# MLP's first product for 14 of 16 token blocks by seven products on pairs of blocks

## The chip, the cores and the metric

One core of a Trainium2 chip runs the whole kernel, a layer with a normalisation, a state space scan, a gelu MLP and a second, FP4-quantised MLP. The metric is the time on the device in microseconds, as the median of several runs. The engines are TensorE (PE in the profile, with its weight loads PEld), VectorE (DVE), ScalarE (ACT), GpSimd (POOL) and SyncE (SP), which here issues all the DMAs, in order.

## The reference

For 2 x 4096 tokens of 512 channels, in float32 (`_L0_ffn_ref` is the quantised MLP, with widths 512, 1408, 512):

```python
xn = _layernorm(x, axis=-1)
x = x + _L0_attn_ref(xn, ...) + _L0_ffn_ref(xn, w_gate, w_up, w_down)

def _L0_attn_ref(x, A_ssm, B_ssm, C_ssm, D_ssm, scale1, scale2, w1, b1, w2, b2):
    x = x + ssm_scan(rmsnorm(x, scale1), A_ssm, B_ssm, C_ssm, D_ssm)
    h = rmsnorm(x, scale2)
    h = jax.nn.gelu(h @ w1 + b1, approximate=False) @ w2 + b2   # w1 512 x 2048, w2 2048 x 512
    return x + h
```

## The kernel before

The tokens are 64 tiles of 128. The first 1742 us do the quantised MLP and the scan and leave two things in DRAM: r_Z (a tile's residual and second MLP) and r_Y (the scan's result). Then comes the MLP stage, the one that changes. Its tokens are 16 blocks of 512 (NB), and its weights are 16 pieces of 128 hidden channels. Every float32 operand of TensorE is split into a high part (rounded to fp32r) and the remainder, and a product takes three passes (PASSES): high with high, high with low, low with high. `Wp[f][0]` and `Wp[f][1]` are high and low of piece f, with w1's part in `[:, 0]` and w2's in `[:, 1]`, and all 16 pieces stay in SBUF.

In each step n = 16 b + f of a loop over the whole stage, `mlp1(n)` (L880) makes 12 matmuls of 512 columns, 4 pieces of the 512 channels by 3 passes, into bank 7 or 4. ScalarE takes gelu of it into `gf` (`gelu`, L1491). VectorE casts that to G2's high part (L1237) and subtracts to get the low part (L1239, `gelu_parts`). Two steps later `mlp2(n)` (L896) makes 12 matmuls, 4 tiles by 3 passes, into banks 0 to 3, which are summed over a block's 16 steps. After f = 15 `result` (L1250) adds the tile's residual, and SP stores it.

Beside that, each tile of the next block is prepared (`prepare`, at steps set by `mlp_steps`). `pre_load` and `z_load` load x, r_Y and r_Z; VectorE's `tile_add` normalises x and adds Y (L1193, L1197); ScalarE squares it for a sum (`tile_square`, L1456); VectorE's `tile_root` is a chain of 11 one-column operations and one scaling (L1203 to L1209); GpSimd's `tile_z` makes the residual with two sums of 128x512 (L1631, L1634), and tile_root's scaling waits for them. `quadrants` stores the tile to DRAM and loads it back with its 32x32 pieces in other places (four DMAs of 128-byte pieces), so that VectorE's 32x32 transpose (L1221) gives the whole transpose, from which `tile_high` and `tile_low` make hT. Block 0 also waits for each piece's weights: `w_high` on ScalarE (L1450) and `w_low` on VectorE (L1188) split piece n + 2 in step n.

Each engine runs a program in order, written out by hand: a wait of one instruction holds all that stands behind it on the same engine. Semaphores give the order between engines.

## Time and profile before

| | us |
|---|---|
| median of 3 runs | 3132.64 |
| lowest, highest | 3131.24, 3133.47 |
| span of the profiled execution | 3132.1 |
| MLP stage from its third first product to TensorE's last matmul | 1742.8 to 3128.9 |

| stretch | TensorE busy | VectorE | ScalarE | GpSimd |
|---|---|---|---|---|
| MLP stage, 1386.1 us | 1383.8 | 664.4 | 286.0 | 160.8 |
| one block of it, 87.04 us | 87.04 | 42.16 | 17.74 | 10.79 |

The profiled execution's span stands half a microsecond below the median of the runs. A matmul's row in the trace is longer than the distance to the next, since matmuls overlap in the array; so the distance of starts is the cost of one. A row of VectorE or GpSimd that took longer than others of its kind waited inside the instruction. "Idle before" in a row ends with the instruction that released it.

### The profile page before, as it was taken

What the parts mean: (1) busy time and instruction counts of PE and PEld (TensorE: products, weight loads), DVE (VectorE), ACT (ScalarE), POOL (GpSimd) and SP (SyncE); (2) the same over time, 40 slices, a digit from 0 to 9 for tenths busy, and PEclk for the clock granted to TensorE, in tenths of its full rate; (3) what the DMA queues carried; (4) which work ended last, traced back from release to release, by engine and by line L of the source; (5) the groups of instructions that cost most, each with busy time, mean ns of one, the idle gap of its engine ahead of it and who ended that gap; (6) DMA issues with size and microseconds to landing.
All of it is one profiled execution on the core that took longest, in us unless ns stands there. A gap on an engine that the chain in (4) does not pass through costs nothing.

```text
span 3132.1 us, 43122 instructions
## 1 busy us (share of the span) xinstructions
PE 3053.1 (97%) x14861; PEld 2472.6 (79%) x14861; DVE 2040.8 (65%) x4427; ACT 1086.7 (35%) x1910; POOL 1149.5 (37%) x1097
## 2 busy tenths in 40 slices
PE   5899999999999999999999999999999999999999
PEld 3678888888877777777777788888888888888887
DVE  8798898987777776767777754444445444444442
ACT  5345655644544343343422422212222122221221
POOL 7556656655555545545554210110111111111000
PEclk9999999999999999999999999999999999999999
DMA  4133434356766666666644533333333333333320
GB/s 128 44 88 91 116 114 120 95 137 183 181 180 174 161 155 174 159 161 168 168 95 98 128 72 72 75 73 72 77 68 80 75 68 71 72 74 74 71 61 14
DMA packets 865577, 335.58 MB, mean 107 GB/s; under 512 B 680400, under 2 KB 771792, under 8 KB 862800
## 3 DMA queue, kind: packets, MB, share of 16 engines
q1 hardware_dynamic: 865360, 332.83, 43.4%
q8 instruction: 119, 1.95, 0.3%
q14 instruction: 98, 0.80, 0.1%
HBM read 225.21 MB, written 107.51 MB: 106 GB/s over the span
## 4 chain that ended last, share of the span: by engine, by line
PE 70%; DVE 15%; issue 5%; POOL 5%; ACT 2%; DMA 2%; SPq 1%; DVEq 0%; POOLq 0%; ACTq 0%
PE bank L880 22%; PE bank L896 22%; PE bank L757 14%; PE bank L779 7%; DVE qs L1000 3%; POOL qa L1547 2%; DVE qa L1017 2%; PE bank L820 2%; DVE qs L1011 2%; DVE qa L973 2%; POOL qa L1541 1%; DVE qb L1025 1%; PE bank L727 1%; PE bank L828 1%; DVE sg L965 1%
## 5 line engine op out<-in xcount | busy, mean ns | idle before, releaser
L880 PE MATMUL bank<-hT,Wp 128*128 128x512 f32 x3072 | 739.6, 390 | 2.2 <-DVE Wp L1188 2.2
L896 PE MATMUL bank<-Wp,G 128*128 128x512 f32 x3072 | 737.6, 389 | 0.0
L880 PEld LDWEIGHTS bank<-hT,Wp 128*128 128x128 f32 x3072 | 577.5, 188 | 122.6 <-issue 2.6
L896 PEld LDWEIGHTS bank<-Wp,G 128*128 128x128 f32 x3072 | 576.6, 188 | 119.9
L757 PE MATMUL bank<-XT,Wg 128*128 128x512 f32 (+1 forms) x2148 | 524.6, 393 | 6.8 <-DVE Wd L1032 6.8
L757 PE MATMUL bank<-XT,Wu 128*128 128x512 f32 (+1 forms) x2148 | 515.7, 389 | 15.9 <-DVE sg L965 15.7
L779 PE MATMUL bank<-Wd,HT 128*128 128x512 f32 x2112 | 515.4, 393 | 6.3 <-POOL HT L1555 5.0
L1237 DVE CAST G<-gf 128x512 fp32r<-128x512 f32 x256 | 110.8, 433 | 599.2 <-PE bank L896 580.0
L757 PEld LDWEIGHTS bank<-XT,Wu 128*128 128x128 f32 x2148 | 401.1, 190 | 106.7 <-issue 25.8
L779 PEld LDWEIGHTS bank<-Wd,HT 128*128 128x128 f32 x2112 | 391.9, 188 | 105.6 <-issue 15.4
L757 PEld LDWEIGHTS bank<-XT,Wg 128*128 128x128 f32 x2148 | 398.7, 190 | 95.9 <-DVE Wd L1032 8.8
L1547 POOL TENSOR_TENSOR qa<-qb,qs 128x512 f32<-128x512 f32 (+2 forms) x277 | 308.2, 1113 | 343.8 <-DVE qb L1025 341.4
L1491 ACT ACTIVATE gf<-bank,vec 128x512 f32<-128x512 f32 x256 | 176.3, 689 | 604.6 <-PE bank L880 603.2
L1555 POOL TENSOR_TENSOR HT<-qb,HT 128x512 fp32r<-128x512 f32 (+1 forms) x179 | 229.6, 1283 | 242.3 <-ACT HT L1331 242.1
L1631 POOL TENSOR_TENSOR zx<-zl,b2r 128x512 f32<-128x512 f32 x64 | 88.9, 1389 | 609.7 <-DMA out_dram<-zx 527.9
L1541 POOL TENSOR_TENSOR qa<-qa,qs 128x512 f32<-128x512 f32 (+1 forms) x243 | 262.8, 1082 | 109.2 <-DVE qs L1005 109.2
L1634 POOL TENSOR_TENSOR zx<-zx,xl 128x512 f32<-128x512 f32 x64 | 82.8, 1293 | 505.0 <-DVE xl L1197 504.3
L1331 ACT ACTIVATE HT<-qb 128x512 fp32r<-128x512 f32 (+1 forms) x179 | 112.1, 626 | 413.2 <-DVE qb L979 413.1
L1017 DVE SCALAR_TENSOR_TENSOR qa<-qb,qa 128x512 f32<-128x512 f32 (+2 forms) x149 | 120.7, 810 | 141.0 <-ACT qb L1303 140.8
L1239 DVE TENSOR_TENSOR G<-gf,G 128x512 fp32r<-128x512 f32 x256 | 178.3, 696 | 8.8
L1338 ACT ACTIVATE sg<-bank 128x512 f32<-128x512 f32 (+1 forms) x179 | 105.5, 590 | 204.9 <-PE bank L757 201.4
L1000 DVE TENSOR_REDUCE qs<-qa 128x32 f32<-128x512 f32 (+1 forms) x243 | 165.2, 680 | 8.3
(121 smaller groups left out, 2828.3 us busy)
## 6 DMA issues: line engine op xcount, KB each, us to landing
px<-in_L_attn_x_dram SPq DMA_DIRECT2D x128, 256.0 KB, 3.3
xin<-in_L_attn_x_dram SPq DMA_DIRECT2D x128, 256.0 KB, 3.3
sT<-r_K SPq DMA_DIRECT2D x128, 256.0 KB, 4.2
r_Z<-xin SPq DMA_DIRECT2D x64, 256.0 KB, 2.5
r_U<-ub SPq DMA_DIRECT2D x16, 1024.0 KB, 6.6
sU<-r_U SPq DMA_DIRECT2D x32, 512.0 KB, 5.0
r_Y<-sY SPq DMA_DIRECT2D x16, 1024.0 KB, 5.7
xl<-in_L_attn_x_dram SPq DMA_DIRECT2D x64, 256.0 KB, 3.1
```

The lines of the kernel that those rows point to most:

```text
L757: ins = e.matmul(bk[:, 0:n], W[wh][:, k, :], inputs(xh, w, k), start=(k == 0 and p_ == 0), stop=(k == KD - 1 and p_ == 2))
L779: ins = e.matmul(DNB[t % 4][:], HT[hh][:, w % 2, a * P:(a + 1) * P], Wd[wh][:, f, :], start=(w == first(n) and p_ == 0), stop=(w == last(n ...
L880: ins = e.matmul(bk[:], Wp[f][wh][:, 0, k * P:(k + 1) * P], hT[xh][b % 2][:, k, :], start=(k == 0 and p_ == 0), stop=(k == KD - 1 and p_ = ...
L896: ins = e.matmul(ACC[j][:], G2[gh][:, n % 2, j * P:(j + 1) * P], Wp[f][wh][:, 1, :], start=(f == 0 and p_ == 0), stop=(f == 15 and p_ == 2))
L1000: e.tensor_reduce(s_, blk(job_in(m)), AX, ALU.max, apply_absolute_value=True).then_inc(s_mx, 1)
L1017: e.scalar_tensor_tensor(Aa, Bb, FLOOR, Aa, ALU.max, ALU.add).then_inc(s_t, 1)
L1239: e.tensor_tensor(G2[1][:, n % 2], gf[:, n % 2], G2[0][:, n % 2].bitcast(F32), ALU.subtract).then_inc(s_glo, 1)
L1331: e.activation(HT[0][:, w % 2, 0:n], qb[:, m % 2, 0:n], ACT.Copy).then_inc(s_hh, 1)
L1491: e.activation(gf[:, n % 2], PB[n % 2][:], ACT.Gelu, bias=vec[:, f:f + 1]).then_inc(s_gl, 1)
L1541: e.tensor_tensor(blk(qa[:, m % 4, 0:n]), blk(job_in(m)), bc(qs[:, m % 4, 1, 0:n // 16], n // 16), ALU.mult).then_inc(s_pa, 1)
L1547: e.tensor_tensor(blk(qa[:, m % 4, 0:n]), blk(qb[:, m % 2, 0:n]), bc(qs[:, m % 4, 0, 0:n // 16], n // 16), ALU.mult).then_inc(s_ph, 1)
L1555: e.tensor_tensor(lo, qb[:, m % 2, 0:n], hi.bitcast(F32), ALU.subtract).then_inc(s_hl, 1)
```

## The change

Blocks 0 and 1 (NB1 = 2) keep the old loop. The other 14 blocks become 7 pairs (PAIRS). For a pair and a unit u, which is a pair of weight pieces 2u and 2u + 1, the first product is a 2x2 block product: the weights are A11, A12, A21, A22 (two pieces by two halves of the 512 channels), the activations B11, B12, B21, B22 (two halves of the channels by two blocks of 512 tokens). Strassen's scheme in Winograd's form makes the four results with seven products instead of eight. It needs four sums of weights (S1 to S4) and four of activations (T1 to T4). Each product is 2 k-halves by 3 passes, 6 matmuls.

**Weights.** In steps 3 to 25 sixteen rounds (`combine_steps`) make the eight weight operands: load of w1, scaling by scale2 on ScalarE, four 128x128 sums on GpSimd (`combine_sums`), high parts on ScalarE (`combine_high`, 128x1024), remainders on GpSimd (`combine_low`, 128x1024), store to r_A in pieces of 512 bytes. There are two buffers wt, one wh and one wl. Later each product's weights, 256 KB, are loaded from r_A into a ring of 14 places.

**Activations.** Each tile is normalised with one unit of the pair before (the first eight in steps 14 to 26, `early_steps`), its residual is summed in place in `zl` and stored to r_Q, the tile to r_N. SP loads two tiles at a time with the pieces moved (`quarters`), VectorE transposes (`conv_turn`), sums into banks (`conv_sums`), ScalarE converts, VectorE and GpSimd subtract (`conv_low`). For a later pair all that lies in `rest`; for the first it lies in steps 26 to 33.

**A unit.** Seven products go into banks 4 to 7, several of them into a bank that is read between two products; VectorE adds the parts (u2, u3, and three results), ScalarE takes four gelus. Between the products stand pieces of the even block's second product for the unit before, into banks 0 to 3. The odd block's second product can't have a bank meanwhile, so its gelus are kept in SBUF and it gets a stretch of its own, `rest`: 16 parts for it and the last 2 of the even block, into banks 4 to 7. The remainder of a gelu's cast moves from VectorE to GpSimd (`second_rest`), and there are three buffers for it. Bank 0 to 3 are scratch for the sums of the next pair once the even block's results are out.

```diff
@@ mlp_steps: the old loop ends with block 1
+    if b + 1 >= NB1:
+        return []
...
+STEPS = ((A11, B11, 4), (S2, T2, 5), (S3, T3, 6), (A12, B21, 4), (S1, T1, 7), (A22, T4, 6), (S4, B22, 7))
+OPENS = (0, 1, 2, 4)
+SECOND = [(0, f) for f in range(14)] + [(1, 0), (1, 1), (0, 14), (0, 15)] + [(1, f) for f in range(2, 16)]
...
+def combine_steps(n):
+    return [k for k in range(16) if 3 + 4 * k // 3 == n]
+def early_steps(n):
+    return [(OLD + r, part) for part in (1, 0) for r in range(8) if 14 + 3 * r // 2 + part == n]
@@ sync_program
+            def unit(c, u):
+                g, o = 8 * c + u, OLD + 8 * (c + 1) + u
+                more = c + 1 < PAIRS
+                for k in range(7):
+                    if g + 2 < 8 * PAIRS:
+                        e.wait_ge(s_p, 7 * g + k + 1)
+                        ring_load(7 * (g + 2) + k)
+                    if u == 7 and k == 1 and more:
+                        quarters(c + 1, 0)
+                    if k == 2 and more:
+                        store_sum(o)
...
+                    if k == 4 and more:
+                        store_normed(o)
+                        z_load(o + 1)
+                    if k == 5 and more and u < 6:
+                        pre_load(o + 2)
...
+            combine_load(0)
+            combine_load(1)
-            for n in range(2, 16 * NB + 2):
+            for n in range(2, 16 * NB1 + 2):
                 if n == 2:
                     z_out(NT - 2)
                     z_out(NT - 1)
+                for k in combine_steps(n - 2):
+                    combine_store(k)
+                for k in combine_steps(n - 1):
+                    combine_load(k + 2)
@@ tensor_program
+            def product(c, u, k):
...
+                elif k == 0:
+                    e.wait_ge(s_gc, 5 * (g - 1) + 2)
...
+                elif k == 5:
+                    e.wait_ge(s_add, 5 * g + 2)
+                elif k == 6:
+                    e.wait_ge(s_add, 5 * g + 3)
+                e.wait_ge(d_ring[q % 14], RING_0 + 16 * (q // 14 + 1))
+                for kt in range(2):
+                    for p_, (xh, wh_) in enumerate(PASSES):
+                        ins = e.matmul(bank[bk][:], ring(q)[:, 256 * wh_ + P * kt:256 * wh_ + P * kt + P],
+                                       combined(b, xh)[:, kt], start=(k in OPENS and kt == 0 and p_ == 0),
+                                       stop=(kt == 1 and p_ == 2), skip_group_check=True)
...
+            def unit(c, u):
+                after = [[(0, 0)], [(0, 1)], [(0, 2), (0, 3)], [(1, 0)], [(1, 1)], [(1, 2)], [(1, 3)]]
+                for k in range(7):
+                    product(c, u, k)
+                    if u:
+                        for a, j in after[k]:
+                            second(c, 2 * (u - 1) + a, j)
@@ vector_program
+            def second_part(c, i):
...
+                if q >= 3:
+                    e.wait_ge(s_m2, used((q - 3) // 32, (q - 3) % 32))
...
+                e.tensor_copy(second_high(q), gelued(half, f)).then_inc(s_gh, 1)
+            def conv_sums(c, i):
...
+                e.tensor_tensor(ba[:, 0:256], HB[:, 0:256], HA[:, 0:256], ALU.subtract).then_inc(s_ts, 1)
+                e.tensor_tensor(ba[:, 256:512], HB[:, 256:512], HB[:, 0:256], ALU.subtract).then_inc(s_ts, 1)
+                e.wait_ge(s_ts, n + 1)
+                e.tensor_tensor(bb[:, 0:256], HB[:, 256:512], ba[:, 0:256], ALU.subtract).then_inc(s_ts, 1)
+                e.wait_ge(s_ts, n + 3)
+                e.tensor_tensor(bb[:, 256:512], HA[:, 256:512], bb[:, 0:256], ALU.subtract).then_inc(s_ts, 1)
+            def unit(c, u):
+                if u:
+                    second_part(c, 2 * u - 1)
+                if c + 1 < PAIRS:
+                    tile_add(o)
...
+                e.tensor_tensor(u2[:], bank[5][:], s1[:], ALU.add).then_inc(s_add, 1)
...
+                e.tensor_tensor(u3[:], bank[6][:], u2[:], ALU.add).then_inc(s_add, 1)
+                if c + 1 < PAIRS:
+                    tile_root(o)
+                second_part(c, 2 * u if u < 7 else 14)
...
+                e.tensor_tensor(gelued(1, 2 * u + 1), bank[7][:], u3[:], ALU.add).then_inc(s_add, 1)
+            def rest(c):
+                for i in range(16, 32):
+                    second_part(c, i)
+                    if i in (17, 18, 24, 26) and more:
+                        conv_turn(d, (17, 18, 24, 26).index(i))
+                    if i == 19:
+                        for j in range(4):
+                            sum_out(c, j)
+                    if i in (20, 21, 25, 28) and more:
+                        conv_sums(d, (20, 21, 25, 28).index(i))
+                    if i in (22, 23, 27, 29) and more:
+                        conv_low(d, (22, 23, 27, 29).index(i))
@@ scalar_program
+            def combine_high(k):
+                e.wait_ge(s_wsum, WSUM0 + 4 * (k + 1))
+                if k:
+                    e.wait_ge(d_wa, WA_0 + 32 * k)
...
+                e.activation(wh[:], wt[:, k % 2], ACT.Copy).then_inc(s_wah, 1)
@@ gpsimd_program
+            def combine_sums(k):
+                w = [wt[:, k % 2, i] for i in range(8)]
+                e.wait_ge(s_wsc, WSC0 + 2 * (k + 1))
+                e.tensor_tensor(w[S1], w[A21], w[A22], ALU.add).then_inc(s_wsum, 1)
+                e.tensor_tensor(w[S3], w[A11], w[A21], ALU.subtract).then_inc(s_wsum, 1)
...
+            def combine_low(k):
+                e.wait_ge(s_wah, WAH0 + k + 1)
+                e.tensor_tensor(wl[:], wt[:, k % 2], wh[:].bitcast(F32), ALU.subtract).then_inc(s_wal, 1)
+            def second_rest(c, i):
+                e.wait_ge(s_gh, q + 1)
+                e.tensor_tensor(second_low(q), gelued(half, f), second_high(q).bitcast(F32), ALU.subtract
+                                ).then_inc(s_gw, 1)
```

**Order on TensorE, inside the MLP stage.** Before, the end of one first product (L880) and the start of a second product (L896), where twelve stand in a row of each:

```order
L880 MATMUL bank<-hT,Wp_1 128x512
L880 MATMUL bank<-hT,Wp_0 128x512 x2
L880 MATMUL bank<-hT,Wp_1 128x512
L880 MATMUL bank<-hT,Wp_0 128x512
L896 MATMUL bank<-Wp_0,G 128x512
L896 MATMUL bank<-Wp_1,G 128x512
```

Now, inside a unit (L1193 is `product`, its weights in the ring `Wp_1`, its activations in HC or WH; L1215 is `second`):

```order
L1193 MATMUL bank<-HC,Wp_1 128x512 x6
L1215 MATMUL bank<-Wp_0,G 128x512
L1215 MATMUL bank<-Wp_1,G 128x512
L1215 MATMUL bank<-Wp_0,G 128x512
L1193 MATMUL bank<-WH,Wp_1 128x512 x6
```

A run of six now alternates with a run of three, and each has waits of its own.

**Order on GpSimd, in the first steps of the MLP stage.** Before, only the residuals of tiles stand there:

```order
L1555 TENSOR_TENSOR HT1<-qb,HT0 128x256
L1631 TENSOR_TENSOR zx1<-zl,b2r 128x512
L1634 TENSOR_TENSOR zx1<-zx1,xl0 128x512
L1631 TENSOR_TENSOR zx1<-zl,b2r 128x512
L1634 TENSOR_TENSOR zx1<-zx1,xl1 128x512
```

Now, with L2201 to L2206 `combine_sums`, L2210 `combine_low`, L2189 and L2192 `tile_z`:

```order
L2192 TENSOR_TENSOR zx1<-zx1,xl0 128x512
L2201 TENSOR_TENSOR wt<-wt 128x128
L2202 TENSOR_TENSOR wt<-wt 128x128
L2204 TENSOR_TENSOR wt<-wt 128x128
L2206 TENSOR_TENSOR wt<-wt 128x128
L2201 TENSOR_TENSOR wt<-wt 128x128
L2202 TENSOR_TENSOR wt<-wt 128x128
L2204 TENSOR_TENSOR wt<-wt 128x128
L2206 TENSOR_TENSOR wt<-wt 128x128
L2210 TENSOR_TENSOR wl<-wt,wh 128x1024
L2189 TENSOR_TENSOR zx1<-zl,b2r 128x512
L2192 TENSOR_TENSOR zx1<-zx1,xl1 128x512
```

Two rounds of sums and one remainder now stand between the residuals of two tiles.

**Order on VectorE, beside the second products.** Before, a step's cast and remainder, and a tile's transpose and low parts:

```order
L1237 CAST G<-gf 128x512
L1239 TENSOR_TENSOR G<-gf,G 128x512
L1221 STREAM_TRANSPOSE bank<-xl 128x512
L1224 SCALAR_TENSOR_TENSOR hT<-bank,vec,hT 128x128 x4
L1237 CAST G<-gf 128x512
```

Now, in `rest` (L1648 is `second_part`, L1600 `conv_turn`, L1696 `sum_out`, L1616 to L1621 `conv_sums`):

```order
L1648 CAST G2x<-GX 128x512
L1600 STREAM_TRANSPOSE yl<-xl 128x512
L1600 STREAM_TRANSPOSE xl<-yl 128x512
L1648 CAST G<-GX 128x512
L1696 TENSOR_TENSOR zq<-bank,zq 128x512 x2
L1696 TENSOR_TENSOR gf<-bank,gf 128x512 x2
L1648 CAST G<-GX 128x512
L1616 TENSOR_TENSOR bank<-xl,st 128x256
L1617 TENSOR_TENSOR bank<-xl 128x256
L1619 TENSOR_TENSOR bank<-xl,bank 128x256
L1621 TENSOR_TENSOR bank<-st,bank 128x256
L1648 CAST G2x<-GX 128x512
```

The casts that TensorE needs now have results, transposes and sums of the next pair between them, and no remainder.

## Rows read from the trace of the kernel before

**Rows 1.** The page: the span, TensorE's 40 slices, GB/s of all queues.
```profile
span 3132.1 us, 43122 instructions
...
PE   5899999999999999999999999999999999999999
...
GB/s 128 44 88 91 116 114 120 95 137 183 181 180 174 161 155 174 159 161 168 168 95 98 128 72 72 75 73 72 77 68 80 75 68 71 72 74 74 71 61 14
```

**Rows 2.** Stretches: length, busy PE, PEld, DVE, ACT, POOL (x), PEclk, DMA share, GB/s.
```profile
1818.96:1906.00 87.04, 87.04 (x385) 72.07 (x385) 42.16 (x113) 17.74 (x40) 10.79 (x8) 1.00 0.37 73
...
1742.80:3128.90 1386.10, 1383.84 (x6097) 1145.02 (x6095) 664.41 (x1735) 285.99 (x635) 160.80 (x120) 1.00 0.34 70
```

**Rows 3.** Timeline: start us, us, engine, line, op, tiles, count.
```profile
2002.61 2.88 PE L880 MATMUL bank<-hT,Wp 128*128 128x512 f32 x12
...
2005.33 2.88 PE L896 MATMUL bank<-Wp,G 128*128 128x512 f32 x12
2005.53 0.69 ACT L1491 ACTIVATE gf<-bank,vec 128x512 f32<-128x512 f32 x1 [4.75 <-PE bank L880]
```

**Rows 4.** Waits of the MLP stage: us in total, times, longest us.
```profile
ACT gf L1491 <- PE bank L880: 603.2, 144, 4.8
```

**Rows 5.** Groups by shape, 1600 to 3100 us: count, busy us, mean ns.
```profile
L1239 DVE TENSOR_TENSOR G<-gf,G 128x512 fp32r<-128x512 f32 x251 | 174.8, 697 | 8.6
L1491 ACT ACTIVATE gf<-bank,vec 128x512 f32<-128x512 f32 x252 | 173.5, 689 | 585.6 <-PE bank L880 584.2 <-DVE G L1239 1.4
L1237 DVE CAST G<-gf 128x512 fp32r<-128x512 f32 x251 | 108.6, 433 | 577.8 <-PE bank L896 558.6 <-ACT gf L1491 19.1
...
L1221 DVE STREAM_TRANSPOSE bank<-xl 128x512 f32<-128x512 f32 x60 | 43.2, 720 | 0.0
...
L1193 DVE TENSOR_SCALAR xl<-xl,mv,rst 128x512 f32<-128x512 f32 x64 | 36.0, 563 | 0.5 <-DMA xl<-in_L_attn_x_dram 0.5
```

**Rows 6.** Timeline: first and last of the 12 operations of tile_root.
```profile
1939.79 0.14 DVE L1203 TENSOR_SCALAR rs<-rs 128x1 f32<-128x1 f32 x1
...
1941.89 0.49 DVE L1209 TENSOR_SCALAR xl<-xl,rs 128x512 f32<-128x512 f32 x1
```

**Rows 7.** Timeline: GpSimd and VectorE together, at 1938 and at 1761.
```profile
1938.02 1.29 POOL L1631 TENSOR_TENSOR zx<-zl,b2r 128x512 f32<-128x512 f32 x1 [2.15 <-DMA zl<-r_Z]
1938.06 1.80 DVE L1239 TENSOR_TENSOR G<-gf,G 128x512 fp32r<-128x512 f32 x1
...
1761.70 1.43 POOL L1631 TENSOR_TENSOR zx<-zl,b2r 128x512 f32<-128x512 f32 x1 [1.50 <-DMA zl<-r_Z]
1761.91 1.50 DVE L1237 CAST G<-gf 128x512 fp32r<-128x512 f32 x1
```

**Rows 8.** Groups of VectorE by shape, whole run: one line, two kinds of input.
```profile
L1025 DVE SCALAR_TENSOR_TENSOR qb<-qb,qa 128x512 f32<-128x512 f32 x142 | 124.0, 873 | 4.9
...
L1025 DVE SCALAR_TENSOR_TENSOR qb<-bank,qa 128x512 f32<-128x512 f32 x125 | 84.5, 676 | 3.2
```

**Rows 9.** Groups of GpSimd by shape, whole run.
```profile
L1575 POOL TENSOR_TENSOR kR<-kR,kC 128x128 f32<-128x128 f32 x60 | 27.6, 461 | 4.6
...
L1541 POOL TENSOR_TENSOR qa<-qa,qs 128x256 f32<-128x256 f32 x6 | 3.8, 626 | 2.8 <-DVE qs L1005 2.8
```

**Rows 10.** DMA issues, to 1745 us, then 1742 to 1830: median us to landing.
```profile
r_W<-kE SPq DMA_DIRECT2D x16, 256.0 KB, 3.0
...
zl<-r_Z SPq DMA_DIRECT2D x4, 256.0 KB, 2.9
r_H<-xl SPq DMA_DIRECT2D x4, 256.0 KB, 2.0
xl<-r_H SPq DMA_DIRECT2D x16, 64.0 KB, 2.5
```

**Rows 11.** Timeline: TensorE's stall after a weight remainder; SP's four pieces.
```profile
1761.53 4.58 PE L880 MATMUL bank<-hT,Wp 128*128 128x512 f32 x12 [2.22 <-DVE Wp L1188]
...
1762.83 2.61 SPq L595 DMA_DIRECT2D xl<-r_H  x4
```

More of the change, by code:

```diff
@@ L266, in build @@
         yl1 = sbt(mctx, "yl1", [P, D])
-        for f in (8, 9, 10, 0, 1, 2, 3, 4, 5, 6, 7):
+        for f in (8, 9, 10):
+            piece(f)
+        with ExitStack() as later:
+            WH = sbt(later, "WH", [P, 8, 4 * D], F32R)
+        for f in range(8):
             piece(f)
@@ new lines, in rest @@
+            def rest(c):
+                more = c + 1 < PAIRS
+                if more:
+                    quarters(c + 1, 1)
+                residual_in(c, 2)
+                residual_in(c, 3)
+                for i in range(4):
+                    tile_result(c, i)
+                for i in range(4, 8):
+                    residual_in(c, i)
+                if more:
+                    quarters(c + 1, 2)
+                    quarters(c + 1, 3)
+                if c + 2 < PAIRS:
+                    pre_load(OLD + 8 * (c + 2))
+                    pre_load(OLD + 8 * (c + 2) + 1)
+                for i in range(4, 8):
+                    tile_result(c, i)
@@ L601, in prepare @@
                     return
[L602 removed]
+                if part == 0:
                     z_load(t + 1)
@@ new lines, in second @@
+            def second(c, i, j):
+                half, f = SECOND[i]
+                q = 32 * c + i
+                for p_, (gh, wh_) in enumerate(PASSES):
+                    if p_ == 0 and (j == 0 or i >= 30):
+                        e.wait_ge(s_gw, q + 1)
+                    if p_ == 0 and f == 0 and half == 0:
+                        if c:
+                            e.wait_ge(s_ev, 8 * (c - 1) + j + 1)
+                        else:
+                            e.wait_ge(s_o, OLD)
+                    if p_ == 0 and f == 0 and half == 1:
+                        g = 8 * c + 7
+                        if j == 0:
+                            e.wait_ge(s_gc, 5 * g + 2)
+                        else:
+                            e.wait_ge(s_add, 5 * g + (1, 4, 5)[j - 1])
+                    ins = e.matmul(bank[4 * half + j][:], (second_high(q), second_low(q))[gh][:, j * P:(j + 1) * P],
+                                   Wp[f][wh_][:, 1, :], start=(f == 0 and p_ == 0), stop=(f == 15 and p_ == 2))
+                if j == 3 and i != 30:
+                    ins.then_inc(s_m2, 1)
+                elif f == 15:
+                    ins.then_inc(s_ac2, 1)
@@ new lines, in unit, with rest @@
+            def unit(c, u):
[5 more added lines that the diff above has]
+                            second(c, 2 * (u - 1) + a, j)
+            def rest(c):
+                for i in range(14, 30):
+                    for j in range(4):
+                        second(c, i, j)
+                for j in range(4):
+                    second(c, 30, j)
+                    second(c, 31, j)
@@ L914, in tensor_program @@
             window(NW + 1)
-            for n in range(2, 16 * NB + 2):
-                if n < 16 * NB:
+            for n in range(2, 16 * NB1 + 2):
+                if n < 16 * NB1:
                     mlp1(n)
@@ L920, in tensor_program @@
                 mlp2(n - 2)
+            for c in range(PAIRS):
+                for u in range(8):
+                    unit(c, u)
+                rest(c)
         def vector_program(e):
@@ new lines, in sum_out, with rest @@
+            def sum_out(c, i):
+                if i % 4 < 3:
+                    e.wait_ge(s_ac2, 6 * c + 3 * (i // 4) + i % 4 + 1)
+                else:
+                    e.wait_ge(s_m2, used(c, 17 if i < 4 else 31))
+                e.wait_ge(d_zq[i % 4], ZQ_0 + 16 * (2 * c + i // 4 + 1))
+                e.tensor_tensor(residual(i), bank[i][:], residual(i), ALU.add).then_inc(s_ev, 1)
+            def rest(c):
+                d = c + 1
+                more = d < PAIRS
+                for i in range(16, 32):
[3 more added lines that the diff above has]
+                    if i == 19:
+                        for j in range(4):
+                            sum_out(c, j)
[3 more added lines that the diff above has]
+                        conv_low(d, (22, 23, 27, 29).index(i))
+                for j in range(4, 8):
+                    sum_out(c, j)
@@ L1292, in vector_program @@
                     prepare(t, part)
+                for o, part in early_steps(n):
+                    (tile_add, tile_root)[part](o)
+            for c in range(PAIRS):
+                for u in range(8):
+                    unit(c, u)
+                rest(c)
         def scalar_program(e):
@@ L1640, in gpsimd_program, with rest @@
+            def rest(c):
+                for i in range(16, 32):
+                    second_rest(c, i)
+                    if i in (17, 20, 25, 27) and c + 1 < PAIRS:
+                        conv_low(c + 1, (17, 20, 25, 27).index(i))
             for m in range(NJ + 3):
```

443 lines of the change are left out of this document (407 added, 36 removed).

## The prediction

> **What bounds the kernel now.** Read the 40 slices of the page first: TensorE stands at 9 in all but the first two [rows 1]. The stage that the change touches is the last 1386 us, from 1742.8 to 3128.9. There TensorE is busy 1383.8 of 1386.1 us, VectorE 664, ScalarE 286, GpSimd 161, the DMA engines a third of the time, at a granted clock of 1.00, which is the 2.4 GHz level [rows 2]. The timeline shows why no other engine matters: a group of 12 matmuls starts every 2.72 us, first product and second product in turn, with no gap at the border [rows 3]. One matmul of 512 columns thus costs 2.72/12 = 0.2267 us (the 0.39 us of a row overlaps the next). The list of waits has its longest total here: ScalarE's gelu waits 603 us for TensorE, up to 4.8 us at a time [rows 4]. TensorE itself waits once in the stage, 2.22 us, below. So each matmul less is worth 0.2267 us, as long as nothing comes late.
>
> **Matmuls removed.** A pair of blocks had 2 x 16 x 12 = 384 matmuls in its first product. Now it has 8 units of 7 products of 2 k-halves by 3 passes, 336. The second product keeps its 384. Seven pairs: 7 x 48 = 336 fewer, 336 x 0.2267 = **76.2 us less**. The transposes of activations in this stage are not on TensorE before or after.
>
> **Inside a unit.** Times are from a unit's start; a product takes 1.36 us, a piece of second product 0.68 or 1.36: in units 1 to 7, 66 matmuls, 14.96 us. Consumers start 0.43 us after the last matmul's start (12 matmuls from 2002.61, the last at 2005.10, gelu at 2005.53 [rows 3]), VectorE's a little later. VectorE: cast to 0.7, the tile's add (0.56 + 0.69 [rows 5]), at worst behind one GpSimd op of 1.29, u2 by 4.9, u3 by 6.4, root chain to 9.0 (11 small ops in 2.1 us, then 0.49) [rows 6], cast to 9.6, sum into bank 7's reader at 10.5 to 11.2; TensorE needs u3 at 10.9 for product 5 and that last sum at 12.9 for product 6. Nothing is late. Unit 0 has no second product beside it, 9.5 us: there product 6 wants the sum at 8.16, but VectorE does u3 to 5.0, the root chain to 7.65, cast to 8.1, sum to 8.8. That is 0.7 and a hop, 0.9 us, in the six pairs that prepare a next one: **+5**. The weight ring is 14 products deep and reloaded two units ahead; 7 x 256 KB and four or five transfers of the tile per 15 us is about 210 GB/s, while slices of the kernel before moved up to 183 without a full queue [rows 1], so I cost it at nothing; with that cover gone it would be tenths of a us per product.
>
> **GpSimd and VectorE share something.** In the timeline at 1938 a VectorE op with two SBUF inputs that starts 0.04 us after a GpSimd op takes 1.80 instead of 0.69, ending 0.55 after GpSimd's end; at 1761.9 a cast takes 1.50 instead of 0.43, ending 0.28 after it [rows 7]. The same line L1025 averages 873 ns with both inputs in SBUF and 676 with one in a bank [rows 8]. So ops of GpSimd and such ops of VectorE (two SBUF inputs, or a cast or scaling from SBUF to SBUF) come one after the other, and readers of a bank are free. Before this costs nothing, because GpSimd has 10.8 us of work per block of 87 [rows 2]. The change gives it much more, so this is the price to work out.
>
> **Blocks 0 and 1, with the weight sums beside them.** Steps are 5.44 us. From step 3 to step 26 (127 us) GpSimd gets 16 rounds of four 128x128 sums (0.46 each) and one 128x1024 remainder (2.38, on the line through 0.46, 0.62, 1.29 for 128, 256 and 512 columns) [rows 7, 9], 67 us, and 12 tiles by 2 x 1.29, 31 us. VectorE holds the same path for 0.28 of a cast and 0.55 of a two-input op [rows 7]: 24 x 0.83 for gelu parts, 24 x 0.55 for weight remainders, 12 x 1.2 for tiles (two scalings 0.28, one two-input op 0.55, small ops), 47 us. Together 145 in 127 us. ScalarE's conversion waits for GpSimd, and the gelu behind it in its queue has 10.88 - (2.9 + 0.69) = 7.3 us of slack [rows 3, 5]; so even a port without an idle moment leaves TensorE 145 - 127 - 7 = 11 us late. Two loops are not without idle moments. The z tile of a pair is a single buffer: load 2.9, two sums 2.6, store 2.0, issues 0.7 [rows 10], 8.2 us plus a hold of about 1, against the 8.16 us that 1.5 steps give, eight times; and one buffer of high parts must be stored (3.0, the nearest row is r_W [rows 10]) before the next conversion. I add 15: **+26**. Bounds: 0, were the sums late without anyone waiting; above, VectorE's own work per step (cast 0.43, remainder 0.69, two weight remainders 1.38, a third of a tile's 6.1) is 4.5, and with all of GpSimd's 4.1 in its way 8.6, so 3.2 x 22 - 7 = 63. Port and loops have the better evidence, so I stay nearer to the lower end.
> The queue ahead of it: the two first loads of sums stand before the last r_Z stores on SP, and the chain r_Z, GpSimd, VectorE, weight remainder already stalls TensorE 2.22 us at 1761.5 [rows 11]. Two loads of 256 KB, of which one alone lands in 2.9 us [rows 10], at about 1 us each in a row: **+2** (0 to 4).
> The pair that follows block 1: its last quarter is turned in step 32, after the remainders of gelu(31), then sums, five conversions, remainders. Laid end to end this ends 9 to 10 us after step 32 begins, when TensorE has 5.44 us of work: **+5** (3 to 15; the upper end if SP, which needs 2.61 us to issue the four pieces of one tile and so 5.2 per quarter [rows 11], is late).
>
> **The own stretch of the second product.** 216 matmuls, 49 us per pair. Each of its 16 parts must be cast (0.43) and subtracted (1.29) in the 5.2 us between the release of its buffer and its use, so VectorE may be 3.4 us late. It is also given 8 transposes (0.72 [rows 5]), 16 half sums (0.43), 12 remainders and 8 results: about 33 us with the casts, and GpSimd 29 us. Going through the queue, parts 21, 22, 26 and 30 come 0.3 to 1.1 us late, because a half sum waits for GpSimd and then the cast for both: 2.4 us; some of it falls on gaps, I take 2 by six pairs, **+12** (0 to 36). The last results and stores after the last matmul are as many as before, at no change.
> The Trainium skill (GPSIMD Engine Reference, 4.1 Engine selection) says that two-input elementwise work belongs on VectorE, GpSimd being about twice slower; rows agree (1.29 against 0.69). By that rule the remainders' move to GpSimd is what loads the shared path, and the 12 us would be near 0 had they stayed; the sum would read 3094.
>
> **Sum.** 3132.1 - 76.2 + 5 + 26 + 2 + 5 + 12 = 3105.9 on the profiled execution; the median of the runs lies 0.5 above its span, so **3106.4**.
>
> **Rivals.** *All covered* (0.22): the rounds of sums have no one waiting in time, holds fall into gaps, only unit 0 and the handover cost, 3132.6 - 76.2 + 5 + 3 = 3064 to some 3085. For it: VectorE and ScalarE idle more than half of the stage [rows 2]. Against: orders are fixed, a wait of one blocks all behind it. *Late quarters* (0.08): in the second stretch VectorE waits in its queue for pieces of 128 bytes that SP issues in 5.2 us per two tiles [rows 11]; if they land 4 us later than the 2.5 of [rows 10], each pair loses 6 instead of 2: 3106 + 24 to 3140. The Trainium skill (DMA: Bandwidth & Descriptors, Specifications) wants at least 512 bytes per piece. The trace shows 2.5 us to landing with pieces of 128 bytes, in a lightly loaded queue. *VectorE bound, slower* (0.10): in blocks 0 and 1 each small op of the root chain meets another GpSimd op, VectorE takes 8.6 us per step, TensorE follows: 3106.4 + 63 - 26 = 3143. It turns slower than before once these blocks lose more than 52 us, 2.4 us per step. *Broken cadence, not what it says* (0.05): groups are now 3 and 6 matmuls with a wait each instead of 12; if a border costs 0.08 us, some 110 per pair make 60 us and 3166. Against: borders between groups of 12 with two or three waits cost 0 [rows 3]. *Forecast* (0.55): 3085 to 3126.
>
> A measurement of this kernel can tell 0.2%, 6.3 us, from no change. Faster than 3126.4 (forecast, all covered and a little of the late quarters): 0.80; within: 0.07; slower: 0.13. The range that leaves out less than two in ten is 3070 to 3136.
>
> **What would show it.** Twelve matmuls in 2.72 us inside a unit (else the cadence fails). Units 1 to 7 of 14.96 us, unit 0 about 10.4, waiting before product 6 for the sum after the root. In blocks 0 and 1 GpSimd busy about 90%, small VectorE ops of 0.5 to 2 us, TensorE idle some 28 us in all, waits naming gelu or conversions. In the own stretch 49 us plus about 2, waits for GpSimd's remainder. The prediction is wrong if these blocks take under 190 us or over 215, or if rest stretches exceed 53.

## The result and the profile after

The changed kernel takes 3200.8 us (median of four runs, 3198.2 to 3203.5) where the kernel before takes 3132.6 beside it: a ratio of 1.0217, 95% interval 1.0204 to 1.0230. It is 68 us slower; 3106.4 and a range of 3070 to 3136 were forecast. Sign and range are both wrong. The working below is on the profiled executions, 3197.4 us against 3132.1, so 65.3 us are to be found. Of all executions one, of e11 below, ran at a granted clock of 0.565 and took 5004 us; it stands in no figure here.

The page of the kernel after: span, TensorE's busy tenths in 40 slices, its granted clock.

```profile
span 3197.4 us, 44061 instructions
...
PE   5899999999999999999999666899999999999999
...
PEclk9999999999999999999999878999999999999999
```

Before, all slices but the first two stood at 9 [rows 1]. Now slices 23 to 26, which are blocks 0 and 1 of the MLP, stand at 6, 6, 6 and 8, and the granted clock dips with them. The rest is as full as before. Four of the ten stretches by windows, and their sum from 1740 to 2040 (length, busy time of PE, PEld, DVE, ACT, POOL with counts, granted clock, DMA share, GB/s):

```profile
1740.00:1760.00 20.00, 18.96 (x84) 15.39 (x82) 9.02 (x24) 5.66 (x12) 1.27 (x1) 1.00 0.75 211
1760.00:1790.00 30.00, 21.51 (x72) 16.46 (x72) 18.41 (x28) 6.98 (x12) 17.01 (x17) 0.83 0.45 121
...
1850.00:1880.00 30.00, 12.89 (x49) 9.66 (x48) 12.69 (x20) 8.10 (x19) 9.96 (x9) 0.76 0.51 128
1880.00:1910.00 30.00, 23.65 (x91) 18.62 (x89) 14.59 (x38) 5.91 (x13) 11.58 (x16) 0.90 0.72 172
...
sum 300.00, PE 205.67 PEld 160.50 DVE 157.00 ACT 80.50 POOL 118.47; mean PE 20.57 PEld 16.05 DVE 15.70 ACT 8.05 POOL 11.85
```

No engine is full there. GpSimd, forecast at 90%, is busy 10 to 17 of 30 us in each stretch from 1760 to 2000, and 118 of the 300. So something other than an engine's full load sets the time. Measured from the trace by the starts of matmuls:

| part | before | after | forecast | difference |
|---|---|---|---|---|
| blocks 0 and 1, first mlp1 to first product, 769 starts | 182.6 | 302.3 | 190 to 215 | +119.7 |
| 336 matmuls less, at 0.2267 | | | -76.2 | -76.2 |
| eight units of the first pair (113.56 without a wait) | | 119.99 | 113.6 + 0.9 + 5 | +6.4 |
| eight units of pairs 2 to 6 | | 114.01 each | 114.5 | +0.45 each |
| own stretches (49.64 without a wait) | | 50.9 to 52.7 | 51.6 | +13.4 in six |

-76.2 + 119.7 + 6.4 + 2.3 + 13.4 = 65.6, which is the 65.3 within rounding. All but one of the lines came out near their forecast; one line, blocks 0 and 1, holds the whole miss. "Without a wait" is the number of matmuls times 0.2267. Against an unbroken cadence these blocks lose 128.3 us (before: 8.5, of which 4.4 are matmuls of the stage ahead that stand between the first groups, as they do now): 99.9 in 23 gaps of more than 1 us, and 27.7 in 138 matmuls that start 0.3 to 1 us after the one before, by median 0.427, where 0.2267 is the cadence.

The list of waits, 1730 to 2035 (us in total, times, longest):

```profile
ACT wh L1981 <- DMA r_A<-wl: 115.5, 14, 16.2
POOL wl L2210 <- ACT wh L1981: 83.6, 14, 13.0
PEld bank L1142 <- ACT gf L1964: 58.3, 10, 11.0
...
PE bank L1142 <- ACT gf L1964: 38.2, 7, 10.6
ACT wt L1973 <- DMA wt<-in_L_attn_w_dram: 35.3, 8, 11.4
...
PE bank L1142 <- DVE Wp L1527: 27.4, 7, 8.1
```

SP's own waits, 1738 to 2030, begin with its load of the next round's weights, which stands behind the round's remainder:

```profile
SPq L751 <- POOL wl L2210: 88.3, 12, 8.7
```

The stores of a round, from issue to landing:

```profile
r_A<-wh SPq DMA_DIRECT2D x16, 512.0 KB, 4.2
r_A<-wl SPq DMA_DIRECT2D x16, 512.0 KB, 5.2
```

Before, ScalarE's one long wait in this stage was for TensorE [rows 4]; now TensorE waits most for ScalarE's gelu, and ScalarE waits for a store. One turn of the loop, from the timeline (start, us, engine, line, operation):

```profile
1792.54 1.06 ACT L1981 ACTIVATE wh<-wt 128x1024 fp32r<-128x1024 f32 x1 [12.72 <-DMA r_A<-wl]
...
1793.67 2.35 POOL L2210 TENSOR_TENSOR wl<-wt,wh 128x1024 fp32r<-128x1024 f32 x1 [13.05 <-ACT wh L1981]
...
1794.50 1.16 ACT L1923 ACTIVATE Wp<-Wr 128x512 fp32r<-128x512 f32 x2
...
1795.54 0.70 ACT L1964 ACTIVATE gf<-bank,vec 128x512 f32<-128x512 f32 x1
...
1796.05 0.37 SPq L751 DMA_DIRECT2D wt<-in_L_attn_w_dram  x1
...
1796.46 0.47 SPq L695 DMA_DIRECT2D xl<-in_L_attn_x_dram  x1
...
1796.71 4.89 PE L1142 MATMUL bank<-hT,Wp 128*128 128x512 f32 x12 [6.93 <-DVE Wp L1527]
...
1796.97 2.57 SPq L699 DMA_DIRECT2D yl<-r_Y  x2
...
1799.59 1.02 SPq L759 DMA_DIRECT2D r_A<-wh  x1
1800.65 2.00 SPq L759 DMA_DIRECT2D r_A<-wl  x1
...
1806.31 1.06 ACT L1981 ACTIVATE wh<-wt 128x1024 fp32r<-128x1024 f32 x1 [6.34 <-DMA r_A<-wl]
```

Read it as a ring. Conversion 1.1, GpSimd's remainder 2.4, SP's issues that stand ahead of the stores in program order (a load of weights, xl, two pieces of yl) 3.5, the high store's issue 1.0, and from the low store's issue to its landing 5.7: 13.8 us from one conversion to the next. The program asks for one in 4/3 steps, 7.25 us; 16 turns at 6.5 too many make 105 us. This turn is not an odd one: the 16 conversions stand 14.8 us apart in the mean. The conversion stands in ScalarE's queue ahead of the next gelu, and ahead of the high part of block 0's next weight piece (L1923), whose remainder the 6.93 us of this turn are waiting for; neither can start while it waits. And the group after a stall takes 4.89 us instead of 2.88: its granted clock is 0.56, and its matmuls start 0.427 us apart, which is the 1.2 GHz level. The trace of before had one such restart, 4.58 us after a 2.22 us stall [rows 11].

### The profile page after: what moved, and what is told of

It is laid out like the page before. It is cut to its first block and busy times, and to the rows that moved or that the text cites. A ratio compares the mean times of both kernels' runs of the same rounds, so it can differ in the third digit from the quotient of the medians.

```text
span 3197.4 us, 44061 instructions
## 1 busy us (share of the span) xinstructions
PE 3016.1 (94%) x14525; PEld 2427.6 (76%) x14525; DVE 2179.4 (68%) x4455; ACT 1156.7 (36%) x1930; POOL 1599.9 (50%) x1457
## 5 line engine op out<-in xcount | busy, mean ns | idle before, releaser
L1019 PE MATMUL bank<-XT,Wu 128*128 128x512 f32 (+1 forms) x2148 | 516.4, 390 | 15.3 <-DVE sg L1304 14.8
L1215 PE MATMUL bank<-Wp,G 128*128 128x512 f32 x1800 | 456.9, 391 | 5.3 <-POOL G L2226 5.2
L1193 PE MATMUL bank<-HC,Wp 128*128 128x512 f32 x1680 | 423.5, 391 | 2.8 <-POOL WH L2219 2.8
L1215 PEld LDWEIGHTS bank<-Wp,G 128*128 128x128 f32 x1800 | 336.9, 188 | 79.7 <-POOL G L2226 10.5
L1193 PEld LDWEIGHTS bank<-HC,Wp 128*128 128x128 f32 x1680 | 316.8, 189 | 68.7 <-POOL WH L2219 3.2
L2226 POOL TENSOR_TENSOR G<-gf,G 128x512 fp32r<-128x512 f32 x75 | 103.3, 1378 | 301.6 <-DVE G L1648 301.6
L1215 PE MATMUL bank<-Wp,G2x 128*128 128x512 f32 x888 | 229.2, 391 | 3.3 <-POOL G2x L2226 3.3
L1215 PEld LDWEIGHTS bank<-Wp,G2x 128*128 128x128 f32 x888 | 166.2, 188 | 39.9 <-POOL G2x L2226 5.8
L1142 PE MATMUL bank<-hT,Wp 128*128 128x512 f32 x384 | 115.5, 460 | 81.3 <-ACT gf L1964 38.2
L1193 PE MATMUL bank<-WH,Wp 128*128 128x512 f32 x672 | 171.3, 391 | 5.0 <-DVE GX L1674 2.6
```

The source lines that it names most:

```text
L1019: ins = e.matmul(bk[:, 0:n], W[wh][:, k, :], inputs(xh, w, k), start=(k == 0 and p_ == 0), stop=(k == KD - 1 and p_ == 2))
L1142: ins = e.matmul(bk[:], Wp[f][wh][:, 0, k * P:(k + 1) * P], hT[xh][b % 2][:, k, :], start=(k == 0 and p_ == 0), stop=(k == KD - 1 and p_ = ...
L1193: ins = e.matmul(bank[bk][:], ring(q)[:, 256 * wh_ + P * kt:256 * wh_ + P * kt + P], combined(b, xh)[:, kt], start=(k in OPENS and kt == 0 ...
L1215: ins = e.matmul(bank[4 * half + j][:], (second_high(q), second_low(q))[gh][:, j * P:(j + 1) * P], Wp[f][wh_][:, 1, :], start=(f == 0 and ...
```

## The experiments

Theory *loop*: the ring above sets the time. Theory *port*: GpSimd's work on the path that it shares with VectorE does. All kernels are timed against the kernel before on the same chip (3132.4 to 3133.5); not all stand on one chip. "Lost" is what a profiled execution's matmuls lose against 0.2267 us each up to the first product.

**e1, no rounds.** combine_load, combine_store, combine_scale, combine_sums, combine_high and combine_low are not called; the ring is filled with other data and the waits are changed to match (as in e2):

```
-                for k in combine_steps(n):
-                    combine_sums(k)
-                for k in combine_steps(n - 1):
-                    combine_low(k)
```

> Left out: all sixteen rounds of weight sums (loads, scalings, sums, conversions, remainders, stores); the ring reads as many bytes from another tensor, so the products have wrong weights. Loop theory (each round goes once around ScalarE's conversion, GpSimd's remainder, SP's stores and their landing before the next may begin, about 14 us, and gelu stands behind it in ScalarE's queue) and port theory (the 145 us of GpSimd and VectorE work that exclude each other) both say: blocks 0 and 1 fall from 302 us to about 190, the rest stays, total 3080 to 3095. If it stays above 3150, neither is the cause and the new order of tiles or the ring is.

3086.2 us, ratio 0.985 (0.983 to 0.987); blocks 0 and 1 take 188.1 us, lost 14.1. So everything outside the rounds holds: 47 us faster than the kernel before, and the rounds cost 115 us, more than the whole miss of 94.

**e2, rounds without stores.**

```
-                for k in combine_steps(n - 2):
-                    combine_store(k)
...
-                e.dma_start(ring(q).bitcast(F32), r_A[q // 7 % 8, STEPS[q % 7][0]]).then_inc(d_ring[q % 14], 16)
+                e.dma_start(ring(q).bitcast(F32), r_Z[q % 56]).then_inc(d_ring[q % 14], 16)
...
-                    e.wait_ge(d_wa, WA_0 + 32 * k)
+                    e.wait_ge(s_wal, WAL0 + k)
```

> Left out: the stores of the weight operands and the waits for their landing; all sums, conversions and remainders stay, the ring reads as many bytes from another tensor (wrong weights). Loop theory: without the landing a round takes some 5 us and nobody waits for it, blocks 0 and 1 take 190 to 210 us, total 3085 to 3105. Port theory: GpSimd's and VectorE's work is the same, so blocks 0 and 1 stay at 280 us or more, total above 3175.

3132.8 us, ratio 0.9997 (0.9987 to 1.0007); lost 59.3. Neither theory's number: the stores cost 68 us, and the rounds without them still 47 against e1.

**e3, stores first.** SP issues a round's stores a step earlier, ahead of the loads of weights and of the tile:

```
-                for k in combine_steps(n - 2):
+                for k in combine_steps(n - 1):
                     combine_store(k)
-                for k in combine_steps(n - 1):
                     combine_load(k + 2)
```

> Same work and result; on SP the two stores of a round now stand right behind its remainder, one step earlier and ahead of the tile's stores and loads. Loop theory: 3 to 5 us of SP's own detour leave each of 16 rounds, 50 to 80 us in all: 3120 to 3150. Port theory: no change, 3195 to 3205.

3158.6 us, 1.0082 (1.0067 to 1.0097); lost 87.9. Issuing the stores ahead of SP's other work gives back 42 us, where 50 to 80 were expected. ScalarE's longest wait is now for the next load:

```profile
ACT wt L1972 <- DMA wt<-in_L_attn_w_dram: 58.4, 9, 10.5
...
ACT wh L1980 <- DMA r_A<-wl: 31.7, 5, 8.9
```

**e4, more buffers.** Three wt with the remainder written in place of the sums, two wh, loads one round further ahead, and the stores one step earlier, but behind SP's work for the tile in that step. As the remainder lies in wt, a load must now wait until that buffer's store has landed:

```
-        wt = sbt(mctx, "wt", [P, 2, 8, P])
-        wh = sbt(mctx, "wh", [P, 8, P], F32R)
-        wl = sbt(mctx, "wl", [P, 8, P], F32R)
+        wt = sbt(mctx, "wt", [P, 3, 8, P])
+        wh = [whx, sbt(mctx, "wh", [P, 8, P], F32R)]
...
-                if k >= 2:
-                    e.wait_ge(s_wal, WAL0 + k - 1)
...
+                if k >= 3:
+                    e.wait_ge(d_sl[k % 3], SL[k % 3] + 16 * (k // 3))
```

> Same work and result; two buffers for the high parts, three for the sums with the remainder written in place, so a conversion waits for the store of two rounds before, not of the last. Loop theory: the loop is no longer closed over a landing; blocks 0 and 1 take 195 to 215 us, total 3095 to 3115, faster than the kernel before. Port theory: as before, 3185 or more.

3157.7 us, 1.0074 (1.0057 to 1.0090); lost 86.1. A miss for the loop theory in its simple form. The wait for r_A is gone from the top of ScalarE's list, but the change put a new one on SP, in front of the next load (the last row is SP's own list), and the loads and the tile's z come late in its place.

```profile
ACT wt L1984 <- DMA wt<-in_L_attn_w_dram: 50.7, 9, 10.4
POOL zl L2203 <- DMA zl<-r_Z: 42.6, 6, 13.7
```

```profile
SPq L755 <- DMA r_A<-wt: 39.8, 10, 5.1
```

**e5 and e6, small operations.** To part the engines' time from the waits, all operations of a round work on 8 columns of each matrix, without stores (e5) and with them (e6, where round 0 stays whole). Of e5:

```
-                w = [wt[:, k % 2, i] for i in range(8)]
+                w = [wt[:, k % 2, i, 0:8] for i in range(8)]
...
-                e.activation(wh[:], wt[:, k % 2], ACT.Copy).then_inc(s_wah, 1)
+                e.activation(wh[:, :, 0:8], wt[:, k % 2, :, 0:8], ACT.Copy).then_inc(s_wah, 1)
```

> As e2 (the rounds without stores of the weight parts; the ring of the products is filled with other data), but every operation of a round works on 8 columns of each 128x128 matrix instead of 128: the loads (512 KB of w1 twice halved, one per round), all instructions, all waits and their places in the queues stay. What is left of the rounds is their chain of waits; what goes is the time of GpSimd, ScalarE and VectorE in them and with it the shared path. e2 had 3132.8 and lost 233.4 - 188.1 = 45 us against e1 in blocks 0 and 1. Port theory (GpSimd's 67 us of sums and remainders and the holds that they give to VectorE are the 45): these blocks take 188 to 195 us, the kernel 3086 to 3095. Chain theory (weights loaded late by an SP queue that stands in other waits, and ScalarE's scaling standing in front of the next gelu, are the 45): the blocks take 220 to 233, the kernel 3118 to 3133. In between, each has the share that is read off.

> The changed kernel with both stores of 512 KB per round and their waits, but with the operations of rounds 1 to 15 on 8 columns of each matrix (round 0 whole; the stored weights are then not the sums, and the output not the reference's). It is the store loop alone. Loop theory: a round still needs the high store (4.2), the low store (5.2) and SP's detours, some 10 to 11 of the 14 us, so 16 rounds take 165 us where the steps give 127, and the blocks lose 35 to 50 us against e1: 223 to 238 us, kernel 3120 to 3140. Port theory (the losses are holds that let the stores seem late): 188 to 200 us, kernel 3086 to 3100.

e5: 3097.0 us, 0.989 (0.9873 to 0.9906), lost 25.4, 2 us above what port asked and far from the chain's 3118. e6: 3166.3 us, 1.0106 (1.0089 to 1.0123), lost 93.8, more than the loop theory asked. Of e6, the list of waits and the timeline of the ring, now with next to no work in it:

```profile
ACT wh L1982 <- DMA r_A<-wl: 108.4, 14, 13.5
```

```profile
1839.36 2.28 SPq L759 DMA_DIRECT2D r_A<-wh  x1
...
1841.68 0.58 SPq L759 DMA_DIRECT2D r_A<-wl  x1
1846.70 0.26 ACT L1982 ACTIVATE wh<-wt 128x64 fp32r<-128x64 f32 x1 [7.46 <-DMA r_A<-wl]
1846.87 0.67 ACT L1964 ACTIVATE gf<-bank,vec 128x512 f32<-128x512 f32 x1
...
1853.51 0.26 ACT L1982 ACTIVATE wh<-wt 128x64 fp32r<-128x64 f32 x1 [5.97 <-DMA r_A<-wl]
```

A conversion of 0.26 us waits 7.46 us for a store, and the gelu starts behind it. Four kernels now make a square, in medians:

| | operations small | operations whole | difference |
|---|---|---|---|
| no stores | 3097.0 (e5) | 3132.8 (e2) | 35.8 |
| stores | 3166.3 (e6) | 3200.8 (changed) | 34.5 |
| difference | 69.3 | 68.0 | |

The two causes simply add, within the noise. From e1's 3086.2 (two executions, 7 us apart): loads, waits and places in the queues 10.8, the operations' time about 35, the stores about 68.

**e9, GpSimd's time alone.** e5 with operations of GpSimd behind each round's small ones that nobody waits for:

```
+                for i in range(4 if k else 0):
+                    idle_work(wl[:, i, 8:P], wl[:, i + 4, 8:P].bitcast(F32))
...
+                if k:
+                    idle_work(wl[:, :, 8:P], wl[:, :, 8:P].bitcast(F32))
```

> e5 (rounds without stores, all their operations on 8 columns) with GpSimd's time given back: behind each round's small sums four operations of 128x120 and behind its small remainder one of 128x960, with two SBUF inputs, on data that nobody waits for. The round's own chain stays short; ScalarE's scalings and conversion stay small. e2 - e5 was 36 us. Port theory (GpSimd's time, in its own queue and on the path that it shares with VectorE, costs TensorE the 36): e9 at 3125 to 3137. Chain theory (the 36 come because each round's operations stand one behind the other until its conversion, and the conversion and scalings of full size hold the gelu behind them): e9 within 8 us of e5, 3097 to 3105.

3121.3 us (3116.8 to 3124.6), 0.9959 (0.9945 to 0.9974); lost 47.3. Between the two forecasts, nearer to port: some 24 of the 36 us are GpSimd's time (22 by what the profiled executions lost), the other 12 need the whole chain or ScalarE's share. How it reaches TensorE stands in its timeline:

```profile
1790.54 2.08 POOL L2201 TENSOR_TENSOR wl<-wl 128x960 fp32r<-128x960 f32 x1
...
1791.01 2.16 DVE L1535 TENSOR_TENSOR xl<-xl,yl 128x512 f32<-128x512 f32 x1
...
1793.20 0.63 ACT L1928 ACTIVATE yl<-xl 128x512 f32<-128x512 f32 x1 [3.84 <-DVE xl L1535]
...
1793.83 1.13 ACT L1922 ACTIVATE Wp<-Wr 128x512 fp32r<-128x512 f32 x2
...
1794.47 1.26 POOL L2191 TENSOR_TENSOR zx<-zx,xl 128x512 f32<-128x512 f32 x1
1794.48 2.41 DVE L1526 TENSOR_TENSOR Wp<-Wr,Wp 128x512 fp32r<-128x512 f32 x2 [1.31 <-ACT Wp L1922]
...
1796.43 4.46 PE L1141 MATMUL bank<-hT,Wp 128*128 128x512 f32 x12 [2.01 <-DVE Wp L1526]
...
1800.02 1.79 POOL L2201 TENSOR_TENSOR wl<-wl 128x960 fp32r<-128x960 f32 x1
...
1800.11 1.72 DVE L1291 SCALAR_TENSOR_TENSOR rs<-rs 128x1 f32<-128x1 f32 x1
```

VectorE's add takes 2.16 instead of 0.69 behind 2.08 us of GpSimd. ScalarE's square waits for the add, and the high part of a weight piece (L1922) stands behind the square. Its two remainders on VectorE then meet the tile's own sum on GpSimd (L2191), take 2.41 instead of 1.3, and TensorE stands 2.01 us for the second.

**e7 and e8, one size changed.** Four blocks go the old way instead of two, and the 16 rounds come one in 18.1 us; e8 is the same without rounds:

```
-NB1 = 2
+NB1 = 4
...
-    return [k for k in range(16) if 3 + 4 * k // 3 == n]
+    return [k for k in range(16) if 3 + 10 * k // 3 == n]
```

> One size changed: four blocks instead of two go the old way, and the same 16 rounds come one in 10/3 steps (18.1 us) instead of one in 4/3 (7.25); six pairs instead of seven go by seven products. Matmuls removed: 6 x 48 = 288, 65.3 us. e1 stood 29.8 us over 3132.6 - 76.2 - ... with its 7 pairs (11.7 in the rest stretches, 6.4 at the first pair, some 5 in blocks 0 and 1, the rest in unit 0 and around); with 6 pairs about 28. Loop theory (a round needs 14 us and 7.25 is too short): the rounds cost 0 to 8 us, kernel 3095 to 3105. A price per round whatever the pace (holds that TensorE pays each time): 115 us as in the changed kernel, 3205; or as in e2 47, 3142.

> e7 without the rounds (ring filled with other data), as e1 is to the changed kernel; the output is not the reference's. Both theories: 3132.6 - 65.3 + 28 = 3095, within 3090 to 3100. It is there for e7: the difference of the two is what 16 rounds cost at the slower pace.

e8 3095.6 us, as expected. e7 3118.7 us, 0.996 (0.9946 to 0.9974), lost 39.3 over four blocks against 16.6 in e8. The same 16 rounds cost 23 us instead of 115, so the price is set by the pace, and not by a fee per round; but 23 is more than the 0 to 8 of the loop theory. Most rounds of e7 also lie behind block 0, where no weights are split. That isn't what saves it: the second half of block 0, with splitting, loses 45 us in the changed kernel and 5.5 in e7, and block 1, without any, loses 57 in the changed kernel.

**e10, e11, e12: what is left at the slower pace.** e10 is e7 with e3's order of SP, e11 is e7 with e4's buffers, and e12 is e10 with

```
-    return [k for k in range(16) if 3 + 10 * k // 3 == n]
+    return [k for k in range(16) if 3 + 8 * k // 3 == n]
```

> e7 (four old blocks, rounds at 18.1 us) with SP's stores of a round put straight behind its remainder, ahead of the tile's issues, as e3 is to the changed kernel. In e7 16 rounds cost 23 us. Loop theory: at 18.1 us a round is no longer bound by its store loop but still late now and then where SP's detours fall in (ScalarE waited 3 times, 6.8 us, for r_A); the order takes these away, 5 to 12 us: 3107 to 3114. Port theory: the 23 us are GpSimd's holds, nothing changes: 3116 to 3121.

> e7 with e4's buffers: three for the weights of a round with the remainder in place, two for the high parts, loads a round earlier. Nothing then waits for a store or a load at this pace. Loop theory: 8 to 15 of the 23 us go, 3104 to 3111. Port theory: 3116 to 3121.

> e10 with a round every 8/3 steps (14.5 us) instead of 10/3 (18.1), so that the 16 rounds are done by step 43, before the eight early tiles and the conversions of the first pair begin at step 46. If the cost comes from rounds and early tiles meeting (port, SP, or ScalarE's queue), it is below e10: 3098 to 3106. If it comes from the pace of the loop (14.5 is near the 14 that a round took), it is above e10: 3115 to 3130.

e10: 3112.7 us, 0.9938 (0.9921 to 0.9955), lost 34.8. This is in the loop theory's range. e11: 3118.8 us, ratio 0.995 (0.9934 to 0.9967), lost 39.5, no gain over e7: the loop theory's forecast for it failed. e12: 3106.6 us, 0.9916 (0.9901 to 0.9931), lost 28.4, where 3098 to 3106 were expected if rounds and early tiles got in each other's way, and 3115 or more if the pace alone counted. A faster round, done before the first pair's tiles begin, is better than a slower one beside them: in the last of the four blocks e12 loses 7.1 us, e10 17.1 and e8, without rounds, 7.3. e12 beats both kernels: 27 us under the kernel before and 94 under the changed one. In it the store is all but out of the list of waits, the gelu follows its conversion at once, and what still holds TensorE now and then is a late operation of VectorE:

```profile
ACT wh L1982 <- DMA r_A<-wl: 3.6, 3, 2.0
```

```profile
1824.10 1.06 ACT L1982 ACTIVATE wh<-wt 128x1024 fp32r<-128x1024 f32 x1 [2.40 <-POOL wt L2210]
...
1825.23 2.37 POOL L2214 TENSOR_TENSOR wl<-wt,wh 128x1024 fp32r<-128x1024 f32 x1 [1.17 <-ACT wh L1982]
1826.06 0.70 ACT L1965 ACTIVATE gf<-bank,vec 128x512 f32<-128x512 f32 x1
...
1827.40 3.02 PE L1142 MATMUL bank<-hT,Wp 128*128 128x512 f32 x12 [0.91 <-DVE hT L1563]
```

## Why the prediction was wrong, step by step

**Right.** The cadence: 0.2267 us a matmul also in groups of 3 and 6, with no cost at the borders. Groups of the kernel after from 2041 us on (count, busy us, mean ns, idle before):

```profile
L1215 PE MATMUL bank<-Wp,G 128*128 128x512 f32 x1800 | 456.9, 391 | 5.3 <-POOL G L2226 5.2
L1193 PE MATMUL bank<-HC,Wp 128*128 128x512 f32 x1650 | 414.9, 390 | 0.0
```

So the 76.2 us of matmuls were really saved, and the rival *broken cadence* falls. The own stretches lost 13.4 us where 12 stood, and by the mechanism named, GpSimd's remainders coming late, mostly at parts 21 and 23 of each:

```profile
2164.39 3.03 PE L1215 MATMUL bank<-Wp,G 128*128 128x512 f32 x12 [0.41 <-POOL G L2226]
...
2170.96 4.42 PE L1215 MATMUL bank<-Wp,G 128*128 128x512 f32 x18 [0.71 <-POOL G L2226]
```

The queue ahead of the rounds stood at +2: with their first stall these blocks lost 1.8 us more than before. Unit 0 was forecast at 0.9 a pair and lost 0.45 in pairs 2 to 6. *Late quarters* did not come.

**Right in part by luck: the first pair.** It lost 6.4 where 5 + 0.9 stood. The chain that the prediction named, last quarter to first product, cost 3.1 us that the table counts with blocks 0 and 1 (the 2.83 us of idle below), and 1.7 at the low clock behind it. The other 4.7 are waits before two products of unit 0 and had no term but the 0.9: the next tile's x and Y landed late, VectorE's `tile_add` waited for them (3.7 and 2.3 us), and u2, u3 and the results stood behind it.

```profile
2029.54 8.63 PE L1193 MATMUL bank<-HC,Wp 128*128 128x512 f32 x30 [2.83 <-POOL WH L2219]
2040.54 1.66 PE L1193 MATMUL bank<-WH,Wp 128*128 128x512 f32 x6 [2.37 <-DVE u L1666]
```

**As a whole.** e1, which is the forecast's sum without its rounds, would have read 3106.4 - 26 - 2 = 3078 by the prediction's own terms and measured 3086.

**Wrong: the term "blocks 0 and 1", +26 with an upper bound of 63.** It measured +120 in the same stretch, of which e1 shows 5.5 to be there without rounds. Three steps of it failed.

*The store.* The prediction wrote that one buffer of high parts must be stored, "3.0, the nearest row is r_W", before the next conversion, and laid nothing end to end. The wait in combine_high asks for both stores of the round before, so remainder and low store belong to the ring as well. The nearest row was a transfer of 256 KB [rows 10]; each of these is 512 KB and lands after 4.2 (high) and 5.2 (low). And between remainder and store stand SP's issues for the tile, although the trace of before showed 2.61 us for four pieces [rows 11]. Even with the rows of before and 1.1 for the conversion the ring was 1.1 + 2.4 + 2.6 + 3.0 = 9.1 us or more against 7.25. That is a quarter over its pace, 30 us in 16 turns, nearly all from rows that the prediction had in hand; measured it was 13.8, nearly double. The stores cost 68.0 and 69.3 us by two pairs of kernels. The prediction's 8.2 against 8.16 was worked out for the wrong loop, the z tile's.

*The engines' time.* Port and hold were forecast at 11 us, and within the bound of 63. Measured 34.5 and 35.8, of which 24 are GpSimd's alone. The mechanism [rows 7, 8] was right and its size too low, because it was counted as a sum over a stretch (145 in 127 us) and not as holds on the chains that TensorE waits for, such as the one to a weight remainder in e9. GpSimd was busy only 118 of 300 us, where about 90% was forecast: a shared path need not be full to make others late.

*What stood behind.* The 7.3 us of slack that were set against the port are the gelu's lead over TensorE. A conversion that waits 12.72 or 16.2 us ahead of it is longer than the lead at a single turn, and it waited 14 times, 8 us in the mean. The prediction set the lead against the port alone.

**Missing: a term for the clock.** 138 matmuls after stalls started at a median of 0.427 us, the 1.2 GHz level, and cost 27.7 us of the 128.3; the granted clock of the stretches was 0.76 to 0.90. e1 has 1.1 us of this, e2 15.5, e6 18.5. The row was there, 4.58 for 2.88 behind a 2.22 us stall [rows 11], and the prediction quoted the stall and left out its 1.7 us. The Trainium skill (TensorE: Matmul & The Clock Gate, Part 1) has a matmul of 512 columns start every 426.7 ns while the array is cold. The trace agrees, with its median of 0.427 us.

**Rivals.** *VectorE bound, slower* had the sign and not the mechanism: VectorE was busy 157 of 300 us. The true case, a ring of stores ahead of the gelu, was in none of the rivals, and half of it stood in the prediction as a half sentence, priced within a lump of 15.

**Open.** The stores' 68 us were not parted further: SP's order gave back 42 of them with the same bytes moved, and more buffers as much, but whether both together would do more at NB1 = 2 was not run. Nor was a kernel that stores and waits for no landing, so how the other 26 divide between waiting and the stores' load on the DMA queue is not shown. Of the operations' 36 us, 12 are between ScalarE's share and the chain. The 11 us that e12 loses against e8 all lie in block 0 (19.8 lost there against 9.2) and were not traced further. That more buffers do nothing in e11 fits e7's list, where ScalarE waited for r_A 3 times and 6.8 us in all; it was not tested further. Whether the own stretches would lose nothing with the remainders back on VectorE, as the prediction says, was not run.

## What to carry to other kernels

Before a second job is laid beside a tight loop, write down its ring: every step from one use of a buffer to the next, the issues that its queue does for others in between included, and compare it with the period; if it is longer, the excess is paid at every turn by whatever stands behind the waiting instruction. Then price a stall with its restart, not with its length alone. If the ring can't be shortened enough, slow its period: here two more blocks of the old kind cost 11 us of matmuls, and with the stores issued first the kernel was 94 us faster.
